# Expert weighting of a fused conv and mixture-of-experts block: other engines for the odd token halves, and another order of the steps

## The reference

```python
x = x + conv_sweeps(layernorm_c(x))          # (16, 64, 36, 100) float32
t = tokens(x)                                # 16 x 3600 tokens of 64 channels
n = layernorm_t(t)
p = softmax(n @ router_w + router_b)         # 8 experts
top_p, top_i = top_k(p, 2); top_p /= sum(top_p)
out = n @ expert_w + expert_b                # every expert: 8 x 64 per token
t = t + sum_k top_p[k] * out[top_i[k]]
```

## Time and profile before

| | |
|---|---|
| median of 3 runs | 1349.32 us (1347.2 to 1349.34) |
| profiled execution | 1347.85 us, span 1346.1 us |
| busy over the span | PE 95%, PEld 87%, DVE 60%, ACT 46%, POOL 45% |
| expert stage | from about 918 us on |
| regions | S8 of the first at 957.00 us, of the last but one at 1318.65 us, of the last at 1336.08 us |

### The profile page before, as it was taken

How to read it: one execution, slowest core, us unless ns; L and a number is a source line. 1 busy time by engine, 2 the same in 40 slices (tenths; PEclk the granted TensorE clock), 3 DMA queues, 4 the chain that set the end, 5 groups by cost and what they waited for, 6 DMA issues and landing times.

```text
span 1346.1 us, 34409 instructions
## 1 busy us (share of the span) xinstructions
PE 1284.5 (95%) x11612; PEld 1171.0 (87%) x11612; DVE 812.4 (60%) x1769; ACT 616.5 (46%) x1701; POOL 611.2 (45%) x770
## 2 busy tenths in 40 slices
PE   6899999999999899999999999996999999999997
PEld 4899999999999899999999999995777777777775
DVE  4788878755555422222222222224999999999996
ACT  5567676633333322222210000003777777777774
POOL 2566666400000000000024444443989898989897
PEclk9999999999999899999999999997999999999999
DMA  4111212100000000000002121110001010101011
GB/s 152 46 53 49 73 49 70 48 0 0 0 0 0 0 0 0 0 0 0 0 22 66 66 66 57 55 63 1 27 27 51 26 51 26 50 26 51 26 50 51
DMA packets 15389, 46.96 MB, mean 35 GB/s; under 512 B 2912, under 2 KB 2912, under 8 KB 15328
## 3 DMA queue, kind: packets, MB, share of 16 engines
q1 hardware_dynamic: 15184, 45.76, 9.8%
q10 hardware_dynamic: 144, 0.33, 0.1%
HBM read 31.33 MB, written 14.75 MB: 34 GB/s over the span
## 4 chain that ended last, share of the span: by engine, by line
PE 81%; DVE 7%; issue 5%; ACT 3%; POOL 3%; DMA 0%; DVEq 0%; POOLq 0%; ACTq 0%
PE twin L990 34%; PE twin L907 27%; PE twin L1054 6%; PE twin L1019 5%; PE twin L1068 4%; PE twin L898 2%; PE twin L892 2%; POOL x_in L357 2%; DVE act_buf L835 1%; PE twin L1035 1%; POOL scratch L362 1%; DVE spare L826 1%; DVE parts L770 1%; DVE scratch L826 1%; ACT x_in L505 1%
## 5 line engine op out<-in xcount | busy, mean ns | idle before, releaser
L990 PE MATMUL twin<-kbuf,late 128*128 128x136 f32 (+2 forms) x3940 | 458.1, 280 | 5.0 <-DVE kbuf L738 5.0
L990 PEld LDWEIGHTS twin<-kbuf,late 128*128 128x128 f32 x3940 | 457.9, 192 | 5.3 <-DVE kbuf L738 5.3
L907 PE MATMUL twin<-parts 128*128 128x384 f32 (+2 forms) x2070 | 392.8, 341 | 0.0
L907 PEld LDWEIGHTS twin<-parts 128*128 128x128 f32 x2070 | 370.8, 188 | 2.8 <-issue 2.5
L313 POOL TENSOR_TENSOR act_buf<-kbuf,x_in 128x144 f32 (+1 forms) x198 | 96.8, 489 | 564.5 <-DVE kbuf L744 564.5
L744 DVE SCALAR_TENSOR_TENSOR kbuf<-twin,act_buf 128x144 f32<-128x144 f32 x394 | 121.4, 308 | 337.0 <-PE twin L990 337.0
L1054 PE MATMUL twin<-em,parts 64*128 64x512 f32 x1404 | 225.4, 423 | 0.5 <-ACT scratch L541 0.5
L504 ACT ACTIVATE sqt<-twin 128x384 f32<-128x384 f32 (+1 forms) x90 | 40.4, 449 | 265.2 <-PE twin L1019 262.9
L488 ACT ACTIVATE act_buf<-kbuf 128x144 f32 x196 | 63.2, 323 | 167.4 <-DVE kbuf L744 167.4
L1054 PEld LDWEIGHTS twin<-em,parts 64*128 64x128 f32 x1404 | 121.2, 189 | 14.5 <-issue 3.1
L295 POOL TENSOR_TENSOR x_parts<-x_in,eps_c 128x400 fp32r<-128x400 f32 x66 | 56.4, 855 | 99.6 <-PE twin L892 81.2
(11 more groups left out here) (116 smaller groups left out, 1703.0 us busy)
## 6 DMA issues: line engine op xcount, KB each, us to landing
x_in<-x SPq DMA_DIRECT2D x36, 400.0 KB, 3.6
x_in<-x_col SPq DMA_DIRECT2D x20, 720.0 KB, 4.1
result<-act_buf SPq DMA_DIRECT2D x36, 400.0 KB, 2.9
scratch<-L_conv_w_d ACTq DMA_DIRECT2D x1, 320.0 KB, 4.6
scratch<-L_conv_w_u SPq DMA_DIRECT2D x1, 320.0 KB, 6.3
late<-L_conv_w_r SPq DMA_DIRECT2D x1, 320.0 KB, 6.4
late<-L_conv_w_l SPq DMA_DIRECT2D x1, 320.0 KB, 6.9
ew<-L_ffn_expert_w SPq DMA_DIRECT2D x2, 128.0 KB, 6.4
```

The costliest lines, as they stand in the source:

```text
L907: last = mm(acc[:, lo:hi], vw[:, k, wpart, si], carry[:, cpart, g, lo + s * BG:hi + s * BG], start=first and si == 0, stop=final and si == ...
L990: last = mm(banks[CONV[g]][:, lo * BG:hi * BG], hw[:, k, si], kbuf[:, g, lo + s:hi + s].rearrange("p j b -> p (j b)"), start=si == 0, stop ...
```

## The change

Two lists and ten tables get new values; no function is changed. Tiles 0, 2, 4, 5 (before in neither list) and 11, 12 (before in `ACT_TILES`) become copy tiles, so that every tile but 10 has a plain copy on ScalarE, a product on GpSimd and 16 transposes on TensorE.

```diff
-        ACT_TILES = (10, 11, 12)
-        COPY_TILES = (1, 3, 6, 7, 8, 9)
+        ACT_TILES = (10,)
+        COPY_TILES = (0, 1, 2, 3, 4, 5, 6, 7, 8, 9, 11, 12)
...
-        TURN_AT = [(0, 1), (1, 1), (2, 1), (3, 2), (5, 0)]
-        COPY_AT = [(1, 0), (2, 0), (2, 1), (3, 1), (4, 0)]
-        VAR_AT = [(0, 1), (1, 2), (2, 2), (3, 2), (4, 2)]
-        INV_AT = [(2, 1), (3, 0), (4, 0), (5, 0), (5, 1)]
-        SCALE_AT = [(2, 0), (2, 1), (3, 1), (3, 1), (3, 1)]
-        BACK_AT = [(5, 1), (7, 0), (7, 1), (8, 2), (10, 1)]
-        HIGH_AT = [(5, 1), (6, 0), (7, 1), (8, 1), (12, 0)]
-        LOW_AT = [(6, 0), (7, 0), (8, 0), (8, 2), (11, 2)]
-        STEP_AT = [(6, 2), (7, 0), (7, 0), (7, 1), (8, 0), (8, 1), (8, 1), (8, 2), (9, 2), (10, 1), (10, 2), (10, 2), (11, 1), (11, 1), (11, 1), (12, 0)]
-        EXP_AT = (10, 0)
+        TURN_AT = [(1, 0), (2, 0), (2, 2), (3, 2), (4, 2)]
+        COPY_AT = [(1, 0), (1, 1), (2, 1), (3, 1), (4, 0)]
+        VAR_AT = [(1, 0), (2, 0), (3, 0), (5, 0), (5, 0)]
+        INV_AT = [(1, 1), (3, 0), (4, 0), (4, 1), (5, 0)]
+        SCALE_AT = [(1, 0), (2, 1), (3, 1), (3, 1), (4, 0)]
+        BACK_AT = [(5, 1), (6, 2), (7, 1), (8, 2), (10, 2)]
+        HIGH_AT = [(5, 0), (6, 0), (7, 0), (9, 0), (11, 1)]
+        LOW_AT = [(5, 1), (7, 0), (8, 0), (8, 2), (12, 0)]
+        STEP_AT = [(6, 2), (7, 0), (7, 2), (7, 2), (8, 0), (8, 0), (8, 1), (8, 2), (10, 0), (10, 1), (10, 2), (11, 1), (11, 1), (11, 1), (11, 2), (12, 0)]
+        EXP_AT = (9, 1)
```

## The result

| | before | after |
|---|---|---|
| median of 10 runs | 1347.25 us (1346.23 to 1350.27) | 1352.76 us (1352.13 to 1356.16) |
| after over before | | 1.0043, 95% interval 1.0034 to 1.0052 |
| profiled execution (span) | 1347.85 (1346.1) | 1355.70 (1353.9) |

In the profiled execution after, 2.5 of the 7.85 us lie ahead of the regions: E0 of the first region starts at 931.32 instead of 928.81. The forecast, no change that a measurement can tell, was wrong; the time lies in the stated range, 1.6 us under the 1354.4 us of the slower rival.

What follows compares the result with a forecast made beforehand. A loop through several engines bounds each region, 22.66 us against 22.64. From 1347.85, +0.3 for sixteen loops, +0.25 first region, -0.5 last region give 1347.9; 0.6 for the executions' mean makes 1348.5 us, range 1344 to 1355.

Steps and rivals of the forecast that it cites:

- slower rival: Token rounds without slack: each T comes before its copy and takes 0.73, +0.36 us per loop, 1354.4 us; chance 0.28.
- three legs: Expert-stage region from S8 to next S8, split at T4 and s0: 10.49 + 4.48 + 7.69 = 22.66 us against 22.64.
- leg 2: From T4 through ScalarE and GpSimd to s0 on VectorE: 4.48 us forecast, 4.30 before, with I3 behind O4.
- each round E, S, T takes 0.79 + 0.49 + 0.64 = 1.92: TensorE's four rounds from T0 to T4, each 1.92 us, with T taking 0.64 where it does not wait.
- leg 1: TensorE from S8 to the last token step T4: 10.49 us forecast, 10.65 before.
- the copies' pace: Token step, ScalarE copy, next token step: read as 1.90 us from T1 to T2, nearly TensorE's round of 1.92.
- these two ties: Near-equal times in S8 to T4: TensorE's round (1.92) against the copies' (1.90), and A2's end against S12's start.
- the even case: Whole kernel within 0.2% (2.7 us) of no change, range 1346.5 to 1351.5 us; chance 0.47.
- Leg 3: From s0 through VectorE's queue to A1 and S8: same 17 instructions, 7.69 us again, at most +0.2.
- The end: From the last region's S8 to the end of A, 6.03 us before: 1.4 less, 0.4 taken back, -1.0.
- The first region's +0.25: One longer sum in the first region's path, adding 0.25 us.
- The rule weighed in the prediction: Relieve the most occupied engine first; by it VectorE is the right engine, but the prediction doubted VectorE's total sets the loop.

Runs made afterwards that it cites:

- three products done twice: Changed kernel with VectorE's even-half product done once more, into an unread buffer, ahead of G0, G2 and G3: 1353.22 us, 1.0043 of the kernel before.
- six short sums: Changed kernel with 8 transposes instead of 16 for tiles 0, 2, 4, 5, 11, 12: 1346.97 us, 0.9995 of the kernel before.
- I3 first: Changed kernel with A2 ahead of G1, V3 ahead of G4, I3 ahead of O4, last tile-12 sum in another PSUM bank: 1347.08 us, 0.9991 of before.
- A2 ahead of G1: Changed kernel with VectorE doing the add A2 before the product G1 instead of behind it: 1350.68 us, 1.0025 of the kernel before.
- tiles 4 and 5 short: Changed kernel with 8 transposes instead of 16 for tiles 4 and 5 only: 1350.35 us, 1.0017 of the kernel before.
- old lists, new order: Changed kernel with the tile lists of before but the new order of steps: 1351.62 us, 1.0026 of the kernel before.
- tiles 0, 11, 12 short: Changed kernel with 8 transposes instead of 16 for tiles 0, 11 and 12 only: 1348.91 us, 1.0009 of the kernel before.

## Why the prediction was wrong

Right: what each part removes and adds; that a region is a loop of three legs; that VectorE's and GpSimd's gains lie beside it, which the three products done twice show for VectorE and the six short sums for both together (no run gives work back to GpSimd alone); leg 2 with I3 behind O4 as its cause (4.48 forecast, 4.46 measured, 4.26 with I3 first).

The step that failed is "each round E, S, T takes 0.79 + 0.49 + 0.64 = 1.92", with which leg 1 came to 10.49 instead of 10.66. Two of its four rounds wait.
- T0 to T1 takes 2.00. K0 starts 1.04 us after T0 (1010.15 - 1009.11), where K1 to K3 start 0.91 to 0.94 after their T, so its copy is late for T1. I had taken T1 to T2 as the copies' pace and not looked at T0 to T1, which took 2.04 before (1006.96 - 1004.92).
- T1 to T2 takes 2.06. V0, which needs K0, stands ahead of G1 and A2 in the new order; A2 ends at 1011.83 + 0.68 = 1012.51, and S12, which waits for it, starts at 1012.65 instead of 0.78 after E2, at 1012.58. T1, which waited, takes 0.69 instead of T0's 0.64. A2 ahead of G1 gives 0.10 us of it back.

T0 before the change, then T0, T1, T2 and K0 after it in the last region but two:

```profile
1004.92 0.89 PE L1019 MATMUL twin<-cl_w,act_buf 64*128 64x72 f32 x12
```
```profile
1283.58 0.87 PE L1019 MATMUL twin<-cl_w,act_buf 64*128 64x72 f32 x12
...
1285.49 0.87 PE L1019 MATMUL twin<-cl_w,act_buf 64*128 64x72 f32 x12
...
1287.42 0.88 PE L1019 MATMUL twin<-cl_w,act_buf 64*128 64x72 f32 x12
```
```profile
1284.48 0.49 ACT L504 ACTIVATE sqt<-twin 128x384 f32<-128x384 f32 x1 [0.24 <-PE twin L1019]
```

Both waits go with K0's delay. In the 14 regions that the program runs in a loop, T0 to T1 takes 1.99 to 2.04 in this kernel and the one before; this region and the next are written out behind the loop, K0 starts 0.90 after T0 there, and the rounds take 1.91, 1.93, 1.91 and 1.93, near the 1.92 forecast, with A2 still behind G1. What in the loop holds K0 up is not shown. These two regions take 22.53 and 22.59 us; before they took 22.28 and 22.37, so the change costs 0.2 us there too.

The slower rival named these two ties and T0 to T4 of 7.85 as its point; 7.90 was measured. Its price was too high, since only two rounds lose, not four (and its sum, 1348.5 + 5.8, is 1354.3). I gave it 0.28 and the even case 0.47, although the even case needed every one of the ties to hold; ties read from rows to within 0.05 us are as good as lost where each can only add. That the time falls into the range of 1344 to 1355 says little for the sum: the upper end was laid to take in this rival.

Leg 3, "7.69 us again", is 0.06 longer. Not through G10, as I had feared, but through L3: S4 and S5 make C3 later, H3 ends at 1025.37 + 0.49 = 1025.86, and L3 starts at 1025.89 instead of following s6 at VectorE's pace. With tiles 4 and 5 short it is 7.67.

The end, "about -1.0", failed outright. The timeline of the last sums after the change, S8, S11, S12 on TensorE, then A2 and A3 on VectorE:

```profile
1343.86 0.71 PE L1068 MATMUL twin<-ident,scratch 64*128 64x64 f32 x16 [0.30 <-DVE act_buf L835]
...
1346.97 0.71 PE L1068 MATMUL twin<-ident,more 64*128 64x64 f32 x16 [0.54 <-POOL more L341]
1348.56 1.12 PE L1068 MATMUL twin<-ident,spare 64*128 64x64 f32 x16 [0.88 <-DVE act_buf L835]
```
```profile
1347.72 0.69 DVE L835 TENSOR_TENSOR act_buf<-twin,act_buf 128x512 f32<-128x512 f32 x1 [1.59 <-PE twin L1068]
...
1349.72 0.23 DVE L838 TENSOR_TENSOR act_buf<-twin,act_buf 128x64 f32<-128x64 f32 x1 [1.30 <-PE twin L1068]
```

P11 and P12 do follow faster, but S12 waits for A2 (0.88), A2 for S11: from S8 to the end of A3 1349.95 - 1343.86 = 6.09 us, against 6.03. The wait on the bank stood in the code; in the rows of before P12 was later than A2, so it did not show. With S12 in another bank the same stretch takes 1342.05 + 0.22 - 1337.18 = 5.09.

Part of these differences is the granted clock. S12 to A3 in the kernel after and in the one with three products twice, with the same instructions (columns as in the earlier trace rows):

```profile
1348.56:1349.72 1.16, 1.12 (x16) 0.93 (x16) 0.00 (x1) 0.00 (x0) 0.00 (x0) 0.50 0.00 0
```
```profile
1346.24:1346.99 0.75, 0.71 (x16) 0.57 (x16) 0.00 (x1) 0.00 (x0) 0.00 (x0) 1.00 0.00 0
```

So 0.41 us of the 6.09 are the clock's; at 1.00 the whole stretch takes 1346.99 + 0.23 - 1341.54 = 5.68. Before, the last S12, with 8 transposes, ran at 0.50 too and took 0.73 to A3 where the six short sums take 0.50 at 1.00, so 6.03 stands for 5.80. At one clock the end gained 0.12 instead of 1.0, and the other bank gives 0.59.

The first region's +0.25 was 1.0 from s0 to s0 in the profiled execution (20.84 against 19.89), but nothing in the kernel with A2 first (19.90), whose sums there are the same. The granted clock in the first token steps differs between the two, as the last section shows.

Together, against the sum of the prediction (+0.05 us): legs 16 x (0.17 - 0.02 + 0.06) = 3.4 us, the end 0.9 to 1.1, the first region -0.25 to +0.7: 4.0 to 5.2; measured is 5.5, with an interval of 4.6 to 7.0. What may be left is not explained.

The rule weighed in the prediction (the Trainium skill, Perfetto Trace Analysis, Identifying the Most-Contended Engine) has the most occupied engine optimized first. Taken as a forecast, with VectorE as that engine, it does not hold here: with TensorE's sums as before (six short) and VectorE's load as after, the region is 22.66 us against 22.64, and 1.83 us more of VectorE adds 0.04.

## What to carry to other kernels

Where most engines are nearly full and none is the bound (here 89 to 94% of a region, ScalarE 74%), follow the loop from one step of a region to the same step of the next and price each leg; relieving an engine beside the loop was worth nothing here, and lengthening a step on it cost what its slack didn't cover. In such a schedule each tie is a possible cost and never a gain, so put the forecast on the side of the ties. When a step gets faster, ask of the last one too which wait was hidden behind it.

## What the runs showed of the hardware

The stretch at the hand-over from the sweeps to the expert stage runs at the lower of TensorE's two levels for a time that differs between executions. One window inside that stretch for the kernel before, after and with A2 first, in that order (columns as in the earlier trace rows); just outside them the clock is 1.00:

```profile
924.30:941.20 16.90, 9.20 (x51) 6.47 (x53) 10.92 (x26) 5.84 (x19) 5.63 (x9) 0.50 0.00 0
```
```profile
921.95:945.70 23.75, 15.31 (x94) 11.46 (x93) 13.33 (x32) 11.60 (x35) 9.50 (x16) 0.50 0.00 0
```
```profile
926.20:943.20 17.00, 9.25 (x51) 6.50 (x53) 10.44 (x26) 6.65 (x21) 5.57 (x11) 0.50 0.00 0
```

The first s0 starts at 929.43, 931.94 and 931.38, so the clock comes back 11.9 us after it before the change and with A2 first, and 13.8 us after it in the profiled execution after. Ahead of the fall TensorE ran, before the change, two groups of three transposes with 1.18 and 0.68 us of waiting in front of them; after it the fall comes earlier, among the 52 token matmuls, which follow a wait of 2.05 us in all three. Inside the stretch TensorE waits 5.41 us for the first softmax in all three. The step T2 of the first region, 11.7 us after s0, then E3, after the change and with A2 first:

```profile
943.68 1.40 PE L1019 MATMUL twin<-cl_w,act_buf 64*128 64x72 f32 x12
944.82 1.39 PE L1054 MATMUL twin<-em,parts 64*128 64x512 f32 x6
```
```profile
943.11 0.85 PE L1021 MATMUL twin<-cl_w,act_buf 64*128 64x72 f32 x12
943.76 0.94 PE L1056 MATMUL twin<-em,parts 64*128 64x512 f32 x6
```

At a granted clock of 0.50 (1.2 of 2.4 GHz) T2 takes 1.14 us to the next step, at 1.00 nearly throughout 0.65. The kernels after and with A2 first have the same instructions up to here; the later return of the clock goes with 0.94 us more from the first s0 to the second (20.84 and 19.90), which no edit has a part in.

The 2.5 us ahead of the first E0 go with the clock too. In the window from 24 to 27 us, in the sweeps, it is 1.00 in the profiled executions of four kernels, which have the first s0 at 929.1 to 929.4 (before; old lists, new order; tiles 0, 11, 12 short; three products twice). In the other six it is 0.50 in that window or just ahead of it, and the first s0 starts at 930.6 to 931.9. All ten have the same instructions there. The window before, then after:

```profile
24.00:27.00 3.00, 1.84 (x11) 1.52 (x9) 2.16 (x4) 1.92 (x5) 1.91 (x2) 1.00 0.00 0
```
```profile
24.00:27.00 3.00, 3.00 (x7) 2.34 (x8) 0.52 (x2) 1.33 (x3) 1.98 (x3) 0.50 0.00 0
```
